# One layer of a graph network on one Trainium2 core: row-sum staging of three slots in place of four

## The chip, the core and the metric

The kernel runs on one core of a Trainium2 chip: TensorE (PE) for matrix products, VectorE (DVE), ScalarE (ACT), GpSimd (POOL), SyncE (SP), which here only issues DMAs, and 16 DMA engines. The metric is the device time of one execution in microseconds, lower is better. In this text 1 MB is 1024 KB, as the profile counts a DMA's size.

## What is computed

```python
# x: 8192 x 128, adj: 8192 x 8192, w: 128 x 128, all float32
A = adj + eye(8192)
d = rsqrt(sum(A, axis=1))
h = (A * d[:, None] * d[None, :]) @ x
x = layernorm(x + elu(h @ w), axis=-1)
```

adj is 256 MB. Its rows have to be summed before d is known, and column t of A can only be used in the product once d_t is known, since x is scaled by it.

## The kernel before, in words

adj is cut into 16 x 16 tiles of 512 x 512 (1 MB). Tile (t, u) holds the columns of band t and the rows of band u. A tile's home is a slot of `space` (line 732): 128 partitions, 4 row blocks (BLOCKS) and 23 slots of 512 columns.

The row bands are taken in order. For band r the strip (columns r to 15 of its rows) is loaded. Together with the tiles to its left, which were loaded earlier as column tiles, it completes the row sums; then d_r follows (`row_sum` on DVE line 1079, `power` on POOL line 914, `scale` on DVE line 1087, copies of the scaled x by turns on DVE 1095 and POOL 932). From then on the column tiles (r, u), u > r, are loaded and used at once. Bands 2 to 11 are HALVED: their d comes in two halves, and a part can be started on the first half of the band.

Of the strip, KEPT says which tiles stay: tile (t, u) is kept for u from t + 1 - KEPT[t] to t. Kept tiles ("near") wait in their slots until d_t is known. The others ("far") are only summed, and are read again at the end ("again"). KEPT sums to 58; 78 tiles are read again, in groups of two row bands (`row_groups`).

Far loads go to the staging area, slots 0 to STAGE - 1. Each of the four row blocks of `space` is one staging row of STAGE x 512 columns (line 812), so with STAGE = 4 a load is 128 rows of 2048 columns: 1 MB, 8 KB contiguous in each row. A strip's odd rest (`part`, line 55) goes in narrower loads. A far load waits until ACT has summed the load that had its staging row before (line 887). Near tiles are loaded in groups of WIDTHS adjacent tiles where so many adjacent slots are free (`near_loads`, line 196), else singly with 2 KB runs. Tiles get slots from STAGE to 22, and the scaled x of a band ("home") takes one such slot too. When all strips are in, the staging slots join them (`close_stage`), and three slots go to the residuals at the end.

Every first-time load is summed by ACT (line 949, one instruction for each row block), every tile is transposed in place by DVE in 32 x 32 squares (line 1072), then multiplied on PE (line 1053) in parts of 1 to 4 tiles of one column band, 128 matmuls for a pair. A part accumulates in one of two PSUM sets; DVE adds it to hT (lines 1106 and 1108). A finished row band gets its product with w (line 1028), ELU and the layer norm.

The order on each engine is written out ahead by `plan()`, a planner that steps through time with fixed costs (line 81 and the `offer` calls): it decides which load is issued next (`next_load`: column tiles go first while fewer than FEED tiles are waiting, strip loads otherwise), which tiles form a part (`next_part`), and which homes stay until the rereads (bands from STAY up; the others are dropped and loaded again). SP issues all loads of adj in this order and waits, one after the other, for the slot or staging row of each. On the chip the engines run at their own pace under semaphores; only the order is the planner's.

Of the kernel before, what the change touches and what calls it, by code (L numbers as in the profile page):

```python
# [5 lines left out]
N = 8192  # L6
F = 128
Q = 4
BAND = 512
BANDS = N // BAND  # L10
BLOCKS = BAND // 128
GROUPS = BAND // 32
SLOTS = 23
STAGE = 4
LATE = 3
KEPT = (1, 2, 3, 4, 5, 6, 5, 4, 5, 4, 5, 4, 1, 2, 3, 4)
AHEAD = 2
STAY = 10
WIDTHS = (4, 2)
XN = 1  # L20
HALVED = range(2, 12)
HALF_JOBS = 2
# [1 line left out]
RING = 4  # L24
SETS = 2
MERGE = 4
FEED = 14
FLIGHT = 4
HOLD = 8
EPS = 1e-5  # L30
# [7 lines left out]
def kept_units():  # L38

    return {(t, u) for t in range(BANDS) for u in range(t + 1 - KEPT[t], t + 1)}  # L40

# [6 lines left out]
def strip_items(r, kept):  # L48

    far = [t for t in range(r, BANDS) if (t, r) not in kept]  # L50
    items = []
    if far:
        assert far == list(range(far[0], BANDS))
        x0 = far[0] * BAND
        part = (N - x0) % 2048
        if part:
            nk = 2048 // part
            items += [("far", r, k, min(nk, BLOCKS - k), x0, part) for k in range(0, BLOCKS, nk)]
        items += [("far", r, k, 1, x, 2048) for x in range(x0 + part, N, 2048) for k in range(BLOCKS)]
    near = sorted((("near", t, r) for t in range(r, BANDS) if (t, r) in kept), reverse=True)  # L60
    if r not in HALVED:
        return items + near
    return items + near + [("split", r), ("rest", r)]
# [14 lines left out]
def plan():  # L78
# [3 lines left out]
    kept = kept_units()  # L82
    loads, tiles, groups = [], [], []
    free = [(0.0, n) for n in range(STAGE, SLOTS)]
    free_rows = [(0.0, n) for n in range(STAGE)]
    homes, tenants = [], [[] for _ in range(SLOTS)]
    order = {e: [] for e in ("sp", "act", "pool", "dve", "pe")}
    ready = {e: [] for e in ("act", "pool", "dve", "pe")}
# [15 lines left out]
    normed = {}  # L104
    counts = {"diagonals": 0, "w": 0, "z": 0, "stored": 0, "outs": 0, "residuals": 0}
    at_row, row_todo, rows_done, stage_open = 0, strip_items(0, kept), False, True
    firsts, queued, rest, backlog = [], [], [], 0
    held_diagonals = {}
# [72 lines left out]
    def drop_home(t):  # L181
        release(homes[home_of.pop(t)][1])
# [13 lines left out]
    def near_loads():  # L196

        left = [v for v in row_todo if v[0] == "near"]
        r, slots = left[0][2], sorted(n for _, n in free)
        for w in WIDTHS:  # L200
            if len(left) < w or len(free) < w + 1 or left[0][1] - left[w - 1][1] != w - 1:
# [31 lines left out]
    def next_load():  # L233
# [15 lines left out]
        if pick_row:  # L249
            pick_row = bool(free_rows) if row_todo[0][0] == "far" else len(free) >= 2  # L250
        if firsts and free and (backlog < FEED or not pick_row):
            t, u = firsts.pop(0)
# [63 lines left out]
    def end_row():  # L316

        nonlocal at_row, row_todo, rows_done, backlog
        if rows_done or any(f[1] == at_row for f in firsts):
            return  # L320
        open_band(at_row)
        if at_row not in HALVED:
            pending_x.append(at_row)
        backlog += sum(1 for v in tiles if v[0] == "first" and v[1] == at_row)
        if at_row + 1 < BANDS:
            at_row += 1
            row_todo = strip_items(at_row, kept)
        else:
            rows_done = True
            close_stage()  # L330

    def close_stage():

        nonlocal stage_open
        if stage_open and rows_done and not far_open:
            stage_open = False
            for slot in range(STAGE):
                tenants[slot].append(("stage", 0))
# [41 lines left out]
    def finished(engine, kind, arg):  # L380
# [48 lines left out]
        elif kind == "part":  # L429
# [4 lines left out]
            for i in these:  # L434
# [4 lines left out]
                else:  # L439
                    again_left[t] -= 1  # L440
            if not first_left[t] and (not again_left[t] or t < STAY and not rows_done):
                drop_home(t)
# [180 lines left out]
def gcn_resnorm(nc: bass.Bass, x: bass.AP, adj: bass.AP, w: bass.AP, out: bass.AP):  # L623
# [3 lines left out]
    AX = mybir.AxisListType  # L627

    loads, tiles, homes, tenants, late, jobs, parts, finals, order, turns, _ = plan()

    def nth_of(engine, kind):
# [90 lines left out]
    with ExitStack() as ctx:  # L722
# [6 lines left out]
        def sem(name):  # L729
            return ctx.enter_context(nc.semaphore(name))  # L730
# [20 lines left out]

        x_loaded = [sem(f"x_loaded{n}") for n in range(XN)]
        w_loaded = sem("w_loaded")
        row_loaded = [sem(f"row_loaded{n}") for n in range(STAGE)]
        loaded = [sem(f"loaded{n}") for n in range(SLOTS)]
        rest_loaded = {n: sem(f"rest_loaded{n[0]}_{n[1]}") for n in sorted({signal_of(v)[1] for v in loads if signal_of(v)[0] == "rest"})}
        res_loaded = [sem(f"res_loaded{n}") for n in range(RING)]
# [46 lines left out]
        def home_of(load):  # L804
# [6 lines left out]
            _, _, _, nk, _, wide, row = load  # L811
            return space[:, row, 0:STAGE].rearrange("p n c -> p (n c)")[:, 0:nk * wide].rearrange("p (k c) -> p k c", k=nk)

# [364 lines left out]
```

## Time and profile before

| | |
|---|---|
| median of 3 runs | 1041.64 us (1041.31 to 1044.76) |
| the profiled execution | 1041.38 us |
| its span | 1039.3 us |
| PE busy | 920.9 us (89%) |
| weight loads | 848.4 us (82%) |
| DVE busy | 788.2 us (76%) |
| ACT busy | 671.4 us (65%) |
| POOL busy | 158.9 us (15%) |
| HBM read | 359.73 MB (here 10^6 bytes), 350 GB/s over the span |

Busy times are of one profiled execution. A busy share over the span says little here, since the kernel has stretches with different limits; the rows further down are read stretch by stretch. An idle time in brackets, as [2.02 <-DVE space L1087], is the time that the engine stood still before the instruction, and what released it.

### The profile page before, as it was taken

To read this page: it belongs to the slowest core of one execution; us is meant where nothing else is said; L and a number is where in the kernel's file an instruction comes from. 1 tells how busy PE (TensorE), PEld (TensorE's weight loads), DVE (VectorE), ACT (ScalarE), POOL (GpSimd) and SP (SyncE) were. 2 spreads that over 40 slices of the span, in tenths; PEclk is the share of its full clock that TensorE was granted. 3 is DMA by queue.
4 is the path that set the end of the run, shared out by engine and by line. 5 is a ranking of instruction groups with operands and counts; after the bars stand their busy time and mean duration, and the time that the engine had idled before them with its cause. 6 is when DMAs were issued, how large, how long until landed. Compare 5 with 4: busy or idle time off the path is not lost.

```text
span 1039.3 us, 35837 instructions
## 1 busy us (share of the span) xinstructions
PE 920.9 (89%) x16128; PEld 848.4 (82%) x16128; DVE 788.2 (76%) x675; ACT 671.4 (65%) x1621; POOL 158.9 (15%) x277
## 2 busy tenths in 40 slices
PE   0099389789798998989999999999999999999995
PEld 0065378679698998989999999999999989999994
DVE  0398298397686968879789877999998978866933
ACT  6888798898889888888888888881213126130201
POOL 0200010300301103030312322344000011000000
PEclk9999789899999999999999999999999999999998
DMA  9999999999999999999999999999899979899920
GB/s 386 401 386 411 402 391 402 396 399 399 378 396 384 386 398 391 384 386 402 382 394 399 390 395 382 386 359 355 288 323 324 305 237 329 283 315 318 347 84 21
DMA packets 168696, 366.23 MB, mean 352 GB/s; under 512 B 6624, under 2 KB 33376, under 8 KB 158816
## 3 DMA queue, kind: packets, MB, share of 16 engines
q1 hardware_dynamic: 151504, 355.49, 92.5%
q10 hardware_dynamic: 17040, 8.46, 2.8%
q8 instruction: 126, 2.06, 0.8%
q14 instruction: 26, 0.21, 0.1%
HBM read 359.73 MB, written 4.19 MB: 350 GB/s over the span
## 4 chain that ended last, share of the span: by engine, by line
PE 63%; DMA 19%; SPq 6%; ACT 5%; DVE 4%; POOL 2%; issue 2%; POOLq 0%; ACTq 0%; DVEq 0%
PE p_set L1053 62%; DMA space<-in_adj 17%; SPq L888 5%; ACT space L949 4%; POOL space L932 2%; DVE space L1072 2%; DMA xn<-in_x 1%; PE p_set L1028 1%; DVE space L1087 1%; SPq L878 1%; POOL d L914 1%; DVE hT L1106 0%; ACT space L980 0%; DVE space L1095 0%; DVE stats L1143 0%
## 5 line engine op out<-in xcount | busy, mean ns | idle before, releaser
L1053 PE MATMUL p_set<-space 32*128 32x256 f32 (+3 forms) x16000 | 905.5, 384 | 106.2 <-DVE space L1072 75.3
L1053 PEld LDWEIGHTS p_set<-space 32*128 32x128 f32 x16000 | 833.5, 187 | 175.8 <-issue 120.0
L949 ACT ACTIVATE space<-space 128x512 f32<-128x512 f32 (+2 forms) x744 | 579.5, 780 | 96.7 <-DMA space<-in_adj 87.2
L1072 DVE STREAM_TRANSPOSE space<-space 128x2048 f32<-128x2048 f32 x256 | 577.2, 2289 | 85.2 <-ACT space L949 55.2
L1106 DVE TENSOR_TENSOR hT<-p_set,hT 128x1024 f32<-128x1024 f32 (+1 forms) x95 | 105.7, 1120 | 98.4 <-PE p_set L1053 98.1
L949 ACT ACTIVATION_READ_ACCUMULATOR space<-space 128x1 f32 x744 | 138.7, 186 | 0.0
L972 ACT ACTIVATE space<-space 128x512 f32<-128x512 f32 x16 | 9.9, 622 | 185.3 <-DVE space L1118 185.3
L914 POOL TENSOR_TENSOR d<-deg,minus_half 128x2 f32<-128x2 f32 (+1 forms) x26 | 20.2, 775 | 550.9 <-DVE deg L1079 550.5
L932 POOL COPY space<-space 32x256 f32<-32x256 f32 (+1 forms) x208 | 94.8, 456 | 27.6 <-DVE space L1087 16.3
L939 POOL TENSOR_TENSOR rstd<-var_eps,minus_half 128x4 f32<-128x4 f32 x16 | 19.1, 1194 | 250.0 <-DVE var_eps L1152 249.9
L957 ACT ACTIVATE space<-space 32x512 f32<-32x512 f32 (+1 forms) x40 | 25.1, 628 | 45.3 <-POOL space L921 40.8
L980 ACT ACTIVATE space<-space,shift,rstd 128x128 f32<-128x128 f32 x60 | 24.7, 482 | 31.6 <-DVE shift L1158 31.6
L1087 DVE TENSOR_TENSOR space<-xn,d 128x256 f32<-128x256 f32 (+1 forms) x26 | 24.8, 954 | 17.7 <-POOL d L914 13.0
L1095 DVE COPY space<-space 64x256 f32<-64x256 f32 (+1 forms) x52 | 20.2, 389 | 1.7
L907 POOL TENSOR_TENSOR space<-space,ident 128x512 f32<-128x512 f32 x16 | 20.4, 1276 | 0.2
L1079 DVE TENSOR_REDUCE deg<-sums 128x2 f32<-128x34 f32 (+1 forms) x26 | 5.0, 191 | 19.5 <-ACT space L949 19.3
L1108 DVE COPY hT<-p_set 128x1024 f32<-128x1024 f32 (+3 forms) x6 | 9.5, 1580 | 11.6 <-PE p_set L1053 11.5
L1028 PEld LDWEIGHTS p_set<-ident,hT 128*128 128x128 f32 x128 | 14.9, 191 | 3.6 <-issue 3.6
L1028 PE MATMUL p_set<-ident,hT 128*128 128x128 f32 x128 | 16.4, 281 | 0.9 <-DVE hT L1106 0.9
L1143 DVE BATCH_NORM_STATS2 stats<-space 128x6 f32<-128x128 f32 x64 | 14.0, 281 | 0.6
L1137 DVE SCALAR_TENSOR_TENSOR space<-space 128x512 f32<-128x512 f32 x16 | 11.0, 689 | 2.2 <-ACT space L974 2.2
L1118 DVE TENSOR_TENSOR space<-p_set,d 128x512 f32<-128x512 f32 x16 | 10.4, 675 | 1.5 <-PE p_set L1028 1.3
(17 smaller groups left out, 40.5 us busy)
## 6 DMA issues: line engine op xcount, KB each, us to landing
space<-in_adj SPq DMA_DIRECT2D x303, 1024.0 KB, 12.6
space<-in_adj SPq DMA_DIRECT2D x50, 512.0 KB, 12.1
space<-in_adj SPq DMA_DIRECT2D x8, 768.0 KB, 13.3
xn<-in_x SPq DMA_DIRECT2D x20, 256.0 KB, 12.1
space<-in_x ACTq DMA_DIRECT2D x16, 256.0 KB, 7.9
out_rows<-space ACTq DMA_DIRECT2D x16, 256.0 KB, 9.9
ident<-in_w ACTq DMA_DIRECT2D x1, 64.0 KB, 5.8
```

The costliest lines, as they stand in the source:

```text
L888: sp.dma_start(home_of(load), source(load)).then_inc(arrival(arg), 16)
L907: nc.gpsimd.tensor_tensor(on_diagonal, on_diagonal, ident[:, :].unsqueeze(1).to_broadcast([128, BLOCKS, 128]), ALU.add)\
L914: nc.gpsimd.tensor_tensor(d[:, r, blocks], deg[:, r % 2, blocks], minus_half[:, blocks], ALU.pow).then_inc(d_ready, 1)
L932: nc.gpsimd.tensor_copy(to, own).then_inc(copied_by["pool"], 1)
L949: ins = nc.scalar.activation(view[:, g], view[:, g], ACT.Copy, accum_out=to[:, g:g + 1])
L957: nc.scalar.activation(to, own, ACT.Copy).then_inc(copied_by["act"], 1)
L980: ins = nc.scalar.activation(pos[:, n % RING, b], pos[:, n % RING, b], ACT.Identity, bias=shift[:, n % RING, b:b + 1], scale=rstd[:, n % R ...
L1028: ins = nc.tensor.matmul(p_set[bank][:, i, F * b:F * (b + 1)], hT[:, at:at + 128], w_sb[:, :], start=True, stop=True)
L1053: ins = nc.tensor.matmul(to, xs_chunk(h, b, turn, q), moving, start=first and not turn and b == blocks_of(half).start, stop=last and turn ...
L1072: nc.vector.transpose(slots[slot], slots[slot]).then_inc(tile_turned, 1)
L1087: nc.vector.tensor_tensor(xs_own(h, half), xn[:, h % XN, blocks], d[:, t, blocks].unsqueeze(2).to_broadcast([128, blocks.stop - blocks.sta ...
L1106: nc.vector.tensor_tensor(rows, new, rows, ALU.add).then_inc(product_added, 1)
```

## The change

STAGE goes from 4 to 3. A far load is then at most 128 x 1536 columns: 768 KB, with 6 KB contiguous in each row. There are still four staging rows, one for each row block; their count was STAGE and is now written as BLOCKS. Slot 3 joins the slots for tiles and homes: 20 in place of 19. With it come other settings: KEPT (sum 61 in place of 58, so 75 tiles are read again), WIDTHS (3, 2), STAY 9 and FEED 12. The order on every engine follows from them by `plan()`.

```diff
--- before.py
+++ after.py
@@ -11,12 +11,12 @@
 BLOCKS = BAND // 128
 GROUPS = BAND // 32
 SLOTS = 23
-STAGE = 4
+STAGE = 3
 LATE = 3
-KEPT = (1, 2, 3, 4, 5, 6, 5, 4, 5, 4, 5, 4, 1, 2, 3, 4)
+KEPT = (1, 2, 3, 4, 5, 6, 6, 4, 5, 4, 3, 4, 5, 6, 1, 2)
 AHEAD = 2
-STAY = 10
-WIDTHS = (4, 2)
+STAY = 9
+WIDTHS = (3, 2)
 XN = 1
 HALVED = range(2, 12)
 HALF_JOBS = 2
@@ -24,7 +24,7 @@
 RING = 4
 SETS = 2
 MERGE = 4
-FEED = 14
+FEED = 12
 FLIGHT = 4
 HOLD = 8
 EPS = 1e-5
@@ -52,11 +52,12 @@
     if far:
         assert far == list(range(far[0], BANDS))
         x0 = far[0] * BAND
-        part = (N - x0) % 2048
+        full = BAND * STAGE
+        part = (N - x0) % full
         if part:
-            nk = 2048 // part
+            nk = full // part
             items += [("far", r, k, min(nk, BLOCKS - k), x0, part) for k in range(0, BLOCKS, nk)]
-        items += [("far", r, k, 1, x, 2048) for x in range(x0 + part, N, 2048) for k in range(BLOCKS)]
+        items += [("far", r, k, 1, x, full) for x in range(x0 + part, N, full) for k in range(BLOCKS)]
     near = sorted((("near", t, r) for t in range(r, BANDS) if (t, r) in kept), reverse=True)
     if r not in HALVED:
         return items + near
@@ -82,7 +83,7 @@
     kept = kept_units()
     loads, tiles, groups = [], [], []
     free = [(0.0, n) for n in range(STAGE, SLOTS)]
-    free_rows = [(0.0, n) for n in range(STAGE)]
+    free_rows = [(0.0, n) for n in range(BLOCKS)]
     homes, tenants = [], [[] for _ in range(SLOTS)]
     order = {e: [] for e in ("sp", "act", "pool", "dve", "pe")}
     ready = {e: [] for e in ("act", "pool", "dve", "pe")}
@@ -751,7 +752,7 @@
 
         x_loaded = [sem(f"x_loaded{n}") for n in range(XN)]
         w_loaded = sem("w_loaded")
-        row_loaded = [sem(f"row_loaded{n}") for n in range(STAGE)]
+        row_loaded = [sem(f"row_loaded{n}") for n in range(BLOCKS)]
         loaded = [sem(f"loaded{n}") for n in range(SLOTS)]
         rest_loaded = {n: sem(f"rest_loaded{n[0]}_{n[1]}") for n in sorted({signal_of(v)[1] for v in loads if signal_of(v)[0] == "rest"})}
         res_loaded = [sem(f"res_loaded{n}") for n in range(RING)]
```

## Rows read from the trace of the kernel before

**Rows 1.** The page's 40 slices: busy tenths of PE, of the DMA engines, and GB/s.
```profile
PE   0099389789798998989999999999999999999995
DMA  9999999999999999999999999999899979899920
GB/s 386 401 386 411 402 391 402 396 399 399 378 396 384 386 398 391 384 386 402 382 394 399 390 395 382 386 359 355 288 323 324 305 237 329 283 315 318 347 84 21
```

**Rows 2.** PE's timeline: start, length, line, form, count, [idle before it <-releaser].
```profile
54.45 57.77 PE L1053 MATMUL p_set<-space 32*128 32x256 f32 x768 [54.45 <-DVE space L1072]
133.09 57.71 PE L1053 MATMUL p_set<-space 32*128 32x256 f32 x896 [20.86 <-DVE space L1072]
196.94 6.49 PE L1053 MATMUL p_set<-space 32*128 32x256 f32 x64 [6.14 <-DVE space L1087]
...
213.36 50.38 PE L1053 MATMUL p_set<-space 32*128 32x256 f32 x896 [3.71 <-issue]
...
393.80 60.80 PE L1053 MATMUL p_set<-space 32*128 32x256 f32 x1088 [2.86 <-DVE space L1087]
456.62 3.01 PE L1053 MATMUL p_set<-space 32*128 32x256 f32 x48 [2.02 <-DVE space L1087]
460.31 48.63 PE L1053 MATMUL p_set<-space 32*128 32x256 f32 x896 [0.69 <-POOL space L932]
509.12 83.16 PE L1053 MATMUL p_set<-space 32*128 32x256 f32 x1536 [0.17 <-POOL space L932]
592.63 146.19 PE L1053 MATMUL p_set<-space 32*128 32x256 f32 x2704 [0.35 <-POOL space L932]
...
838.62 7.19 PE L1053 MATMUL p_set<-space 32*128 32x256 f32 x128 [1.46 <-DVE hT L1106]
...
962.62 62.44 PE L1053 MATMUL p_set<-space 32*128 32x256 f32 x1152
1025.97 2.02 PE L1028 MATMUL p_set<-ident,hT 128*128 128x128 f32 x16 [0.91 <-DVE hT L1106]
```

**Rows 3.** Windows: us, busy PE, PEld, DVE, ACT, POOL, clock, DMA share, GB/s.
```profile
592.50:1028.00 435.50, 433.00 (x7824) 408.53 (x7824) 348.14 (x363) 160.46 (x373) 68.73 (x97) 1.00 0.89 305
...
700.00:1028.00 328.00, 325.63 (x5840) 306.54 (x5832) 254.81 (x290) 69.21 (x139) 33.57 (x37) 1.00 0.84 279
```

**Rows 4.** Timeline of all engines around band 6's second half.
```profile
453.69 0.19 ACT L949 ACTIVATION_READ_ACCUMULATOR space<-space 128x1 f32 x1
453.92 0.19 DVE L1079 TENSOR_REDUCE deg<-sums 128x2 f32<-128x34 f32 x1
454.25 0.70 POOL L914 TENSOR_TENSOR d<-deg,minus_half 128x2 f32<-128x2 f32 x1 [2.81 <-DVE deg L1079]
454.99 1.49 DVE L1087 TENSOR_TENSOR space<-xn,d 128x256 f32<-128x256 f32 x1 [0.88 <-POOL d L914]
```

**Rows 5.** Windows, columns as in rows 3: 8 KB packets, then 2 KB.
```profile
12.00:38.00 26.00, 0.00 (x0) 0.00 (x0) 0.00 (x0) 21.13 (x23) 0.00 (x0) 1.00 1.01 420
...
124.60:148.80 24.20, 15.71 (x208) 12.82 (x212) 21.07 (x14) 22.11 (x70) 7.38 (x10) 0.73 1.05 387
```

**Rows 6.** Loads on line 888: two around 330 us, one around 336.
```profile
L888 SPq DMA_DIRECT2D space<-in_adj x2: 847/1705/2563, 329.4 to 330.3; - x2
DMA to landing us min/median/max: 12.6/13.5/14.4
...
L888 SPq DMA_DIRECT2D space<-in_adj x1: 1417/1417/1417, 336.0 to 336.0; - x1
DMA to landing us min/median/max: 14.3/14.3/14.3
```

**Rows 7.** Loads on line 888: five full staging loads of strip 1, then all rereads.
```profile
DMA to landing us min/median/max: 7.7/7.9/7.9
...
DMA to landing us min/median/max: 5.5/8.7/14.1
```

**Rows 8.** Groups by form: ACT's sums; count, busy us, mean ns, idle before.
```profile
L949 ACT ACTIVATE space<-space 128x512 f32<-128x512 f32 x624 | 384.8, 617 | 56.2 <-DMA space<-in_adj 47.0
L949 ACT ACTIVATE space<-space 128x2048 f32<-128x2048 f32 x76 | 145.2, 1911 | 31.1 <-DMA space<-in_adj 31.1
L949 ACT ACTIVATION_READ_ACCUMULATOR space<-space 128x1 f32 x744 | 138.7, 186 | 0.0
L949 ACT ACTIVATE space<-space 128x1024 f32<-128x1024 f32 x36 | 37.7, 1048 | 8.5 <-DMA space<-in_adj 8.5
L949 ACT ACTIVATE space<-space 128x1536 f32<-128x1536 f32 x8 | 11.8, 1472 | 0.8 <-DMA space<-in_adj 0.6
```

**Rows 9.** Groups by form: the one part of a single tile on PE.
```profile
L1053 PE MATMUL p_set<-space 32*128 32x128 f32 x128 | 3.8, 270 | 0.0
```

**Rows 10.** Loads on line 888: issued from 8 to 23 us, first strip.
```profile
DMA to landing us min/median/max: 6.4/9.0/20.3
```

## The prediction

> **What bounds the kernel now.** The plan, read first, says what has to happen: the 16 row strips are read once (256 tiles of 1 MB), which gives the row sums, and a tile of column band t can only be multiplied once d_t is known. 58 of the 136 tiles on or above the diagonal are kept until then, 78 are only summed and read again. The page's slices come next [rows 1]: the DMA engines are full up to about slice 26 (675 us) and move 380 to 410 GB/s, then less, while PE goes from idle to full. So the kernel has a stretch that the transfers set and one that PE sets, and the question is where the one passes into the other.
>
> PE's timeline gives that place [rows 2]: each idle row of PE is a band boundary at which it had no tile left and waited for the next d. They shrink: 54.45 us at the start, 20.86 at band 1, 6.14, 1.39, 0.69 and 3.71 at band 2, then about 4, 3 and 3, and at band 6 2.02 and 0.69. Behind 460 us there are 0.17 and 0.35, one of 1.46 at 838.62 (PE waits for a PSUM set, not for a tile) and 0.91 before the last product. PE is busy 433.0 of the 435.5 us from 592.5 on [rows 3]. So the end is: the time at which the early strips have come in, plus PE's remaining work, plus 11 us behind the last product. A tile read again costs the end its PE work, not its transfer: during the rereads the DMA engines moved 279 GB/s [rows 3].
>
> PE's work per tile is fixed: nine pairs of tiles in 62.44 us are 3.47 us a tile [rows 2]. Three tiles fewer to read again therefore don't take 3 x 3.47 us off the end; the same three are multiplied earlier instead. They help only as far as they fill idle time of PE.
>
> **Part by part.**
> (1) Tiles per band (15 - t column tiles plus KEPT[t]): before 16 for bands 0 to 5, then 14, 12, 12, 10, 10, 8, 4, 4, 4, 4; after the same 16 up to band 5, then 15, 12, 12, 10, 8, 8, 8, 8, 2, 2. Nothing changes for PE ahead of band 6, where some 101 of its 107 us of idle time lie, paced by transfers. Band 6 gains one tile, (6,1): 3.47 us of work, and a second pair of tiles that can be multiplied on the first half of d_6, ahead of the second half. The wait it would fill is the half-band chain at 451 to 457 us: last sum ends 453.9, row sum 0.19, power 0.70, scale 1.49, and PE starts at 456.62 [rows 4]. What is idle from there to 593 is 2.02 + 0.69 + 0.17 + 0.35 = 3.23 us [rows 2], all less than the 3.47 us added. Gain 3.2 us, floor 0 (if the planner puts the pair elsewhere).
> (2) Strips in 6 KB packets. The far loads go from 80 to 110: 80 of 768 KB, 24 of 512 KB (rows 8 to 13), 3 of 768 KB and 3 of 256 KB in 2 KB packets. 8 KB packets moved 420 GB/s, 2 KB packets 387 [rows 5], which is 2.49 and 2.71 us per MB. For 6 KB: tile (4,7) was issued at 330.28 and landed 14.4 us later, at 344.7; the third of the 768 KB loads behind it was issued at 336.0 and landed at 350.3 [rows 6]. Three loads in 5.6 us is 1.87 us each, 2.49 to 2.51 per MB: the same as 8 KB within 1%. Strips 0 to 5 hold 51 MB of far tiles, 48 of them in 6 KB packets: 48 x 0.01 = +0.5 us, and +0.3 for the odd 2 KB band of strips 0, 4 and 5: +0.8, between 0 and 1.5.
> (3) Groups of three kept tiles instead of four. Before, groups of four appeared in strips 0 to 2 alone (all other kept tiles came singly or in pairs at 2 or 4 KB). Three adjacent free slots are easier to find than four; each group of three saves 3 x (2.71 - 2.50) = 0.6 us of transfer and 3 us of ACT, which has cover. Strips 3, 4 and 5 could have one each, strip 1 two in place of four plus one. I take -0.8 us, between 0 and -1.9. With (2) this is 0.
> (4) Staging in flight. A far load waits until ACT has summed the load that had its row before. Four rows of 1 MB run with 7.9 us from issue to landing and the DMA engines full [rows 7]. With 768 KB the four rows turn in 4 x 1.87 = 7.5 us, of which ACT takes 1.47 + 0.19 [rows 8], leaving 5.8 us from issue to landing. The shortest landing of a whole tile is 5.5 us, with 2.71 of it transfer [rows 7], so a 768 KB load can land in about 4.7. It fits with 1.1 us to spare: cost 0.
> (5) ACT's sums of far blocks: 80 x (1.47 + 0.19) + 24 x (1.05 + 0.19) + 12 x 0.80 = 172 us after, against 170 before [rows 8]. ACT isn't the bound.
> (6) The odd tiles. Column 6 has 15 tiles: one part of three. The last reread group has (6,0) alone, as the very last part. A lone tile costs 3.8 us [rows 9] against 3.47: +0.3.
> (7) Reread groups: 4, 4, 4, 12, 14, 18, 19 tiles instead of 8, 8, 10, 14, 18, 20. Each group end asks DVE to add before the output product. Only one such place cost PE time before (1.46 us [rows 2]); more of them cost 0 to 4.4, I take +0.5.
> (8) STAY 9 keeps the scaled x of band 9, one x load less: nothing while PE leads. FEED 12 only shifts when column tiles go ahead of strip loads.
> (9) The price in slots. Kept tiles plus the homes of bands 9 and up hold slots: at the end of strip 10, 12 kept and 2 homes of 20 (before 9 and 1 of 19); at the end of strip 11, 12 and 3 (before 4 and 2). Only 5 slots are then left for streaming, where 13 were. PE is fed from them while strip 11 lands, and band 11 is also reached earlier (153 tiles precede it, not 154), so it has no slack to spend. At the end of strip 9 the kernel before lives on 7 free slots without a gap. I take 0, bounds 0 and +7 (two tiles' work).
>
> Sum on the profiled execution: -3.2 + 0 + 0 + 0.3 + 0.5 = -2.4. The profiled execution took 1041.38 us, its span 1039.3, the median of the runs is 1041.64: forecast 1039.2.
>
> The Trainium skill (DMA: Bandwidth & Descriptors, Bandwidth and Rules for kernel authors) speaks against smaller loads: at least 1 MiB per DMA, and a fixed 2 us for each. The rows above set the step from 1 MB to 768 KB at 2.49 - 1.87 = 0.62 us, a quarter of the load, so nothing fixed shows while loads queue. By the page's fixed part in full, 30 loads more would cost an estimated 60 us.
>
> **Rivals.**
> (a) The streaming slots run out (part 9). PE waits at bands 10 to 12 for tiles that can't be loaded because kept ones hold the slots. For: 5 slots cover 5 x 3.47 = 17 us, and the near tiles of strip 11 with the d chain take about 15. Against: PE is behind the transfers by a few us there. It decides once that stretch exceeds 17 us; price 3.5 to 9 us: 1042.5 to 1048. This is the case that ends slower.
> (b) Staging starves (part 4). If landing needs the 6.4 us that was the shortest in the first strip [rows 10], the four rows turn in 8.1 us instead of 7.5, 0.15 us a load; over the 64 whole far loads of strips 0 to 5 that is 9.6 us, all on the path: 1045 to 1049. Against: most far loads stand between tile loads that cover them.
> (c) Early strips come quicker: the three-wide groups form everywhere and less of the odd loads shows; another 1.5 to 4 us: 1035 to 1037.5.
> (d) The gap is not filled or moves to the next band: no change, 1041 to 1042.
> (e) A fixed cost per load does show: by the shortest landings about 2.8 us, exposed for each far load that is added, 30 x 2.8 = 84 us: 1125.
>
> **How the numbers follow.** About 0.3% (3.1 us) is what a measurement here can tell from no change. Forecast case (1036.5 to 1041) 0.45, of which 0.18 below 1038.5; (a) 0.17, of which 0.12 above 1044.8; (b) 0.08; (c) 0.13, of which nearly all below; (d) 0.14; (e) 0.03. Faster 0.18 + 0.13 + 0.02 = 0.33; slower 0.12 + 0.07 + 0.03 = 0.22; same 0.45. The range 1034.5 to 1047 leaves out (e), the far ends of (b) and (c) and the worst of (a).
>
> **What would show it.** PE's gaps up to band 5 as before within 2 us; no gap at band 6; matmul pitch unchanged; a far stretch at 415 to 420 GB/s with landings near 5.8 us. Wrong if PE has gaps between 590 and 700 us (then a), if the first product or band 1 comes more than 1 us later (b), or if the band gaps ahead of band 6 shrink.

## The result, and the profile after

The kernel after takes 1044.99 us (median), the kernel before 1041.90 in the same comparison; the ratio is 1.003, with a 95% interval of 1.0021 to 1.0039. It is slower by 0.3%, some 3.1 us, where 1039.2 was forecast: inside the range, on the other side of "before". All ratios in this text are of undisturbed executions; one of 2814.92 us with seven rows and one of 1467.42 us with the early table are not among them. The profiled execution took 1044.75 us, its span 1043.0. Lines of the kernel after are one higher than those of before (matmuls L1054, sums L950, loads L889, transposes L1073, scale L1088).

The page's slices of after, as in [rows 1]:

```profile
PE   0089479689798999999999999999999999999995
DMA  9999999999999999999999999989989988999920
GB/s 344 404 387 375 409 389 389 395 397 396 376 383 395 385 397 384 376 393 392 384 385 389 384 389 388 389 305 287 339 299 322 347 296 260 318 307 302 337 99 21
```

The first slice moves 344 GB/s where it moved 386. PE has an 8 in the third slice where it had a 9; from slice 14 on it has no digit under 9 but the last slice's, where before still had an 8 in slices 16 and 18. PE's timeline of after, columns as in [rows 2]:

```profile
56.99 58.38 PE L1054 MATMUL p_set<-space 32*128 32x256 f32 x768 [56.99 <-DVE space L1073]
137.00 57.72 PE L1054 MATMUL p_set<-space 32*128 32x256 f32 x896 [21.63 <-DVE space L1073]
201.85 6.00 PE L1054 MATMUL p_set<-space 32*128 32x256 f32 x64 [7.13 <-DVE space L1088]
209.92 5.38 PE L1054 MATMUL p_set<-space 32*128 32x256 f32 x64 [2.07 <-DVE space L1088]
...
399.88 7.15 PE L1054 MATMUL p_set<-space 32*128 32x512 f32 x64 [1.79 <-DVE space L1088]
407.22 103.02 PE L1054 MATMUL p_set<-space 32*128 32x512 f32 x1648 [0.19 <-DVE space L1088]
510.45 1.15 PE L1054 MATMUL p_set<-space 32*128 32x256 f32 x16 [0.21 <-POOL space L933]
512.84 3.00 PE L1054 MATMUL p_set<-space 32*128 32x256 f32 x48 [1.24 <-DVE space L1088]
516.52 45.18 PE L1054 MATMUL p_set<-space 32*128 32x256 f32 x832 [0.68 <-POOL space L933]
562.14 73.67 PE L1054 MATMUL p_set<-space 32*128 32x256 f32 x1360 [0.44 <-POOL space L933]
636.16 124.44 PE L1054 MATMUL p_set<-space 32*128 32x256 f32 x2048 [0.36 <-issue]
1029.58 2.05 PE L1029 MATMUL p_set<-ident,hT 128*128 128x128 f32 x16 [1.41 <-DVE hT L1107]
```

Against [rows 2]: the first product is 2.5 us later (54.45 to 56.99), band 1 3.9 us (133.09 to 137.00), band 2 4.9, band 5 6.1 (393.80 to 399.88); the end of the last product is 3.6 us later (1027.99 to 1031.63). So the change loses 6.1 us by band 5 and gives 2.5 back behind it. There is no row at band 6 any more. The two windows that this cuts, columns as in [rows 3], first of the kernel before:

```profile
0.00:393.80 393.80, 292.33 (x4737) 256.00 (x4737) 266.25 (x166) 335.44 (x789) 43.32 (x85) 0.95 1.03 394
393.80:1028.00 634.20, 628.59 (x11392) 592.43 (x11392) 514.54 (x481) 331.97 (x825) 113.16 (x190) 1.00 0.93 332
```

and of the kernel after:

```profile
0.00:399.88 399.88, 294.28 (x4736) 260.70 (x4737) 267.27 (x166) 337.46 (x805) 43.24 (x85) 0.94 1.02 388
399.88:1031.60 631.72, 627.19 (x10880) 575.90 (x10880) 513.46 (x488) 326.31 (x839) 112.14 (x189) 1.00 0.93 328
```

Of the 6.1 us ahead of band 5, 4.1 are idle time of PE (393.80 - 292.33 = 101.5, then 399.88 - 294.28 = 105.6) and 2.0 are longer busy time for the same matmuls, at a mean granted clock of 0.94 instead of 0.95 (both are means over stretches at 2.4 and at 1.2 GHz). The transfers of that stretch run at 388 instead of 394 GB/s. Where they fall behind shows at once. The window of 8 to 13 us, first before, then after:

```profile
8.00:13.00 5.00, 0.00 (x0) 0.00 (x0) 0.00 (x0) 5.00 (x10) 0.00 (x0) 1.00 1.01 419
```

```profile
8.00:13.00 5.00, 0.00 (x0) 0.00 (x0) 0.00 (x0) 4.39 (x10) 0.00 (x0) 1.00 0.86 306
```

The fifth load of after waits for ACT's sums of the first. ACT's timeline of after shows when those are done:

```profile
5.61 1.28 ACT L950 ACT_TABLE_LOAD   x1 [5.61 <-DMA space<-in_adj]
6.91 0.63 ACT L950 ACTIVATE space<-space 128x512 f32<-128x512 f32 x1
...
8.66 0.19 ACT L950 ACTIVATION_READ_ACCUMULATOR space<-space 128x1 f32 x1
...
13.32 1.48 ACT L950 ACTIVATE space<-space 128x1536 f32<-128x1536 f32 x1 [0.93 <-DMA space<-in_adj]
```

The first load lands at 5.6 us, the table costs 1.28, three sums of 512 columns follow, and the row is free at 8.85; the fifth load is issued at 8.9 and lands at 13.3, some 3.3 us behind the fourth instead of 1.9. Before, the fifth load was issued later still (9.2), but three rows of 1 MB were in flight behind the first (in after 256 KB and twice 768) and it landed on the beat of 2.49 us. A later stretch, of strip 1's staging loads, shows the same; 97 to 106 us, first before, then after:

```profile
97.00:106.00 9.00, 9.00 (x132) 6.42 (x128) 4.47 (x2) 7.08 (x8) 0.00 (x0) 1.00 1.01 419
```

```profile
97.00:106.00 9.00, 9.00 (x112) 5.64 (x108) 2.90 (x2) 7.43 (x10) 0.00 (x0) 1.00 0.98 369
```

There ACT starts its sums of whole rows 1.87 us apart with one interval of 2.29 in after (98.56 to 100.85 us), and 2.48 apart throughout in before.

The lack shows in the waits of SP's queue too. Queue, line, whom it waited for: us in total, times, longest; before, then after:

```profile
SPq L888 <- PE p_set L1053: 424.2, 94, 8.9
SPq L888 <- ACT space L949: 91.3, 44, 11.2
```

```profile
SPq L889 <- PE p_set L1054: 398.3, 88, 9.9
SPq L889 <- ACT space L950: 151.4, 66, 10.8
```

SP waits 60 us more for a sum to free a staging row, and ACT in turn waits 100.3 instead of 87.2 us for a landing. The HBM reads fell from 359.73 to 356.32 MB: 3.15 for the three tiles that are no longer read again, and 0.26 for band 9's x, which is loaded once less (here 10^6 bytes).

### The profile page after: what moved, and what is told of

Read it like the earlier page. It is cut to its first block, busy times and chain, and to the rows that moved or that the text cites. A ratio compares the mean times of both kernels' runs of the same rounds, so it can differ in the third digit from the quotient of the medians.

```text
span 1043.0 us, 34873 instructions
## 1 busy us (share of the span) xinstructions
PE 921.5 (88%) x15616; PEld 836.6 (80%) x15616; DVE 788.1 (76%) x682; ACT 667.8 (64%) x1651; POOL 157.8 (15%) x276
## 3 DMA queue, kind: packets, MB, share of 16 engines
HBM read 356.32 MB, written 4.19 MB: 346 GB/s over the span
## 4 chain that ended last, share of the span: by engine, by line
PE 72%; DMA 14%; SPq 5%; ACT 3%; DVE 2%; POOL 2%; issue 2%; ACTq 0%; POOLq 0%; DVEq 0%
PE p_set L1054 70%; DMA space<-in_adj 14%; SPq L889 4%; ACT space L950 3%; PE p_set L1029 2%; POOL space L933 1%; DVE space L1088 1%; DVE space L1073 1%; POOL d L915 1%; SPq L879 0%; DVE hT L1107 0%; ACT space L981 0%; DVE stats L1144 0%; DVE space L1138 0%; DVE deg L1080 0%
## 5 line engine op out<-in xcount | busy, mean ns | idle before, releaser
L1054 PE MATMUL p_set<-space 32*128 32x256 f32 (+3 forms) x15488 | 906.1, 392 | 108.7 <-DVE space L1073 78.6
L1054 PEld LDWEIGHTS p_set<-space 32*128 32x128 f32 x15488 | 821.7, 188 | 190.9 <-issue 132.8
L950 ACT ACTIVATE space<-space 128x512 f32<-128x512 f32 (+2 forms) x764 | 582.9, 764 | 110.6 <-DMA space<-in_adj 100.3
L1073 DVE STREAM_TRANSPOSE space<-space 128x2048 f32<-128x2048 f32 x256 | 577.2, 2289 | 92.9 <-ACT space L950 54.8
L1107 DVE TENSOR_TENSOR hT<-p_set,hT 128x1024 f32<-128x1024 f32 (+2 forms) x102 | 108.6, 1079 | 89.3 <-PE p_set L1054 88.8
L950 ACT ACTIVATION_READ_ACCUMULATOR space<-space 128x1 f32 x764 | 142.5, 187 | 0.0
L958 ACT ACTIVATE space<-space 32x512 f32<-32x512 f32 (+1 forms) x30 | 18.8, 628 | 59.7 <-POOL space L922 57.7
L1088 DVE TENSOR_TENSOR space<-xn,d 128x256 f32<-128x256 f32 (+1 forms) x26 | 23.3, 895 | 16.6 <-POOL d L915 12.7
L1109 DVE COPY hT<-p_set 128x1024 f32<-128x1024 f32 (+2 forms) x6 | 9.4, 1568 | 15.4 <-PE p_set L1054 15.4
L922 POOL TENSOR_TENSOR space<-xn,d 128x512 f32<-128x512 f32 x3 | 3.5, 1162 | 61.2 <-DMA xn<-in_x 61.2
```

Of the source, the lines that this page charges most:

```text
L950: ins = nc.scalar.activation(view[:, g], view[:, g], ACT.Copy, accum_out=to[:, g:g + 1])
L1054: ins = nc.tensor.matmul(to, xs_chunk(h, b, turn, q), moving, start=first and not turn and b == blocks_of(half).start, stop=last and turn ...
L1073: nc.vector.transpose(slots[slot], slots[slot]).then_inc(tile_turned, 1)
L1088: nc.vector.tensor_tensor(xs_own(h, half), xn[:, h % XN, blocks], d[:, t, blocks].unsqueeze(2).to_broadcast([128, blocks.stop - blocks.sta ...
L1107: nc.vector.tensor_tensor(rows, new, rows, ALU.add).then_inc(product_added, 1)
```

## The experiments

The theory is rival (b): four rows of 768 KB leave the transfers without work, because a row comes free too late. Its opponents are the odd loads alone, ACT's late start, the order that the planner writes, and a price of the smaller load itself. Times are in us; "band 5" is the start of its first matmul on PE.

Each ratio is to executions of before in the same comparison; the other columns are of one profiled execution each.

| kernel | ratio to before, 95% | first product | band 1 | band 5 | last product ends | last - band 5 |
|---|---|---|---|---|---|---|
| before | 1 | 54.5 | 133.1 | 393.8 | 1028.0 | 634.2 |
| after | 1.003 (1.0021 to 1.0039) | 57.0 | 137.0 | 399.9 | 1031.6 | 631.7 |
| after, nine rows in strip 0 | 0.9999 (0.999 to 1.0008) | 55.2 | 134.6 | 397.3 | 1028.7 | 631.4 |
| after, seven rows everywhere | 0.9967 (0.9956 to 0.9978) | 55.1 | 133.4 | 395.4 | 1026.5 | 631.1 |
| before, six rows | 0.9997 (0.9983 to 1.0011) | 54.6 | 133.4 | 393.7 | 1028.5 | 634.8 |
| after, three rows | 1.042 (1.0401 to 1.0439) | 62.3 | 147.6 | 425.1 | 1072.0 | 646.9 |
| before, three rows | 1.0081 (1.0063 to 1.01) | 58.2 | 140.3 | 402.2 | 1036.8 | 634.6 |
| after, table early | 1.0014 (1.0001 to 1.0027) | 56.4 | 136.3 | 398.7 | 1029.7 | 631.0 |
| before, table early | 0.9999 (0.9986 to 1.0011) | 54.4 | 133.1 | 393.3 | 1028.0 | 634.7 |
| after, nine rows and table early | 0.9999 (0.9988 to 1.0011) | 55.2 | 134.6 | 397.5 | 1028.7 | 631.2 |
| after, nine rows, other costs | 1.0002 (0.9988 to 1.0015) | 55.2 | 135.2 | 398.1 | 1031.4 | 633.3 |
| after, odd part last | 1.0023 (1.001 to 1.0036) | 55.3 | 135.1 | 398.0 | 1032.5 | 634.5 |

### Nine rows in the first strip

```
+ROWS = 9
+    first_far = [k for k, load in enumerate(loads) if load[:2] == ("far", 0)]
+    for n, k in enumerate(first_far):
+        loads[k] = loads[k][:6] + (n % ROWS,)
...
+            if row >= BLOCKS:
+                at = BAND * STAGE * (row - BLOCKS)
+                return hT[:, at:at + nk * wide].rearrange("p (k c) -> p k c", k=nk)
```

> The changed kernel, but the far loads of strip 0 alternate over nine staging rows (four as before, five in hT, which nothing uses until the first product is added). Depth theory (four rows of 768 KB let the transfers run dry in strip 0): the first product comes 1.5 to 2.5 us earlier than the changed kernel's 56.99 us, every band start up to band 5 moves by as much, and the end too: 1042.5 to 1043.5 us. Packet theory (6 KB packets are slower by themselves): nothing moves, 1045. Order theory (the loss comes from the order and the narrow loads, not from waiting for staging rows): nothing moves, 1045.

Measured: 1042.03 us beside 1041.66 of before, ratio 0.9999. The window of 8 to 13 us is full again:

```profile
8.00:13.00 5.00, 0.00 (x0) 0.00 (x0) 0.00 (x0) 5.00 (x11) 0.00 (x0) 1.00 1.02 422
```

The first product is 1.8 us earlier than in after, band 5 2.6, the last product 2.9. Rows in one strip alone take back nearly the whole of the 3.1 us, a little more than expected (1042.5 to 1043.5). The kernel is then even with before, not ahead of it. Of the 6.1 us at band 5 they take back 2.6.

### Three rows, in both kernels

Each far load also waits for the sum of the far load three before it.

```
+    fars = [k for k, load in enumerate(loads) if load[0] == "far"]
+    row_third = {k: fars[n - 3] for n, k in enumerate(fars) if n >= 3}
...
+                if load[0] == "far" and row_third.get(arg) is not None:
+                    sp.wait_ge(act_summed, sum_nth[row_third[arg]])
```

> The changed kernel with one more wait: each far load also waits until the far load three before it is summed, so three are in flight at most instead of four; order and sizes unchanged. Depth theory: a 768 KB load takes 4.4 us to land on idle DMA engines and 1.7 us to be summed, so three rows give one load in 2.05 us at best instead of 1.88; band 5 starts 5 to 12 us later than 399.9 and the end moves with it: 1050 to 1057 us. Packet and order theory: within 1.5 us of 1045.

> The kernel before with the same added wait: three far loads of 1 MB in flight, 3 MB, as many bytes as four of 768 KB. Depth theory, in bytes: it loses about what the changed kernel lost before band 5, 3 to 6 us, so 1044 to 1048 us, and PE's gap at band 6 stays. Packet and order theory: within 1 us of 1041.9.

Measured: after 1085.7 us, ratio 1.042; before 1050.44 us, ratio 1.0081. The sign is that of the depth theory in both. The size was foreseen in neither: before was expected at 1044 to 1048 us, after at 1050 to 1057, and after's loss of 41 us is over four times that of before. PE's timeline of after with three rows, and its window of 8 to 13 us:

```profile
62.28 57.31 PE L1058 MATMUL p_set<-space 32*128 32x256 f32 x768 [62.28 <-DVE space L1077]
147.61 57.40 PE L1058 MATMUL p_set<-space 32*128 32x256 f32 x896 [28.01 <-DVE space L1077]
217.75 6.44 PE L1058 MATMUL p_set<-space 32*128 32x256 f32 x64 [12.74 <-DVE space L1092]
```

```profile
8.00:13.00 5.00, 0.00 (x0) 0.00 (x0) 0.00 (x0) 2.86 (x8) 0.00 (x0) 1.00 0.63 222
```

So the kernel after stands on a slope where one row less costs 4%, and the kernel before nearer to its foot. By the table 25.2 us of after's loss lie ahead of band 5 and 15.2 behind it, where PE goes on waiting at band boundaries up to 673 us; before loses 8.4 and 0.4. Why the wait lasts so long in after wasn't traced.

Before on three rows also tests whether bytes alone count, since it has 3 MB in its rows as after has on four. It loses 8.4 us at band 5, where 3 to 6 were expected and after itself lost 6.1.

### The staging cycle by itself

All but the cycle is left out: SP issues far loads of one width into so many rows, ACT sums each over its row, and SP waits for a sum to free a row. Six stretches, each given by width, rows and number of loads:

```
PHASES = ((2048, 4, 24), (1536, 4, 32), (1536, 5, 32), (1536, 3, 32), (2048, 3, 24), (1024, 4, 48))
...
                if ahead:
                    sp.wait_ge(summed, ahead)
                sp.dma_start(stage[:, r, 0:wide], adj[128 * row:128 * row + 128, col:col + wide]).then_inc(landed[r], 16)
...
                act.wait_ge(landed[r], many)
                nc.scalar.activation(stage[:, r, 0:wide], stage[:, r, 0:wide], ACT.Copy, accum_out=sums[:, k:k + 1]).then_inc(summed, 1)
```

> Only the staging cycle, nothing else of the kernel: loads of 128 rows, each summed by ACT, each waiting for the sum of the load that had its row. Six stretches one after the other: 2048 columns with 4 rows (24 loads), 1536 with 4, 5 and 3 rows (32 each), 2048 with 3 rows (24), 1024 with 4 rows (48). The output is not computed. Depth theory: 2.49 us a load; 1.88 to 1.95; 1.88; 2.05 to 2.3; 2.5 to 2.6; 1.3 to 1.5. Packet theory: 1536 columns take over 1.92 us with 4 and with 5 rows alike. Order theory: 1.88 with 4 rows, so that the cycle by itself loses nothing.

Its windows, one for each stretch in that order (busy ACT and POOL, clock, DMA share, GB/s):

```profile
1.00:62.00 61.00, 46.91 (x47) 0.00 (x0) 1.00 1.00 413
66.00:128.00 62.00, 48.06 (x61) 0.00 (x0) 1.00 1.00 405
132.00:193.00 61.00, 48.63 (x61) 0.00 (x0) 1.00 1.00 412
196.00:273.00 77.00, 48.52 (x61) 0.00 (x0) 1.00 0.91 327
276.00:348.00 72.00, 45.92 (x46) 0.00 (x0) 1.00 0.95 349
352.00:426.00 74.00, 52.90 (x93) 0.00 (x0) 1.00 0.97 340
```

The mean interval between landings and the median time from issue to landing in the steady part of each stretch:

| load | rows | us per load | us per MB | issue to landing |
|---|---|---|---|---|
| 1 MB | 4 | 2.50 | 2.50 | 7.9 |
| 768 KB | 4 | 1.935 | 2.58 | 6.2 |
| 768 KB | 5 | 1.884 | 2.51 | 7.8 |
| 768 KB | 3 | 2.44 | 3.25 | 5.7 |
| 1 MB | 3 | 3.01 | 3.01 | 7.1 |
| 512 KB | 4 | 1.555 | 3.11 | 5.1 |

The smaller load has no price: with five rows 768 KB cost per MB what 1 MB does. With four rows it lags by 0.05 us a load, as an interval of 2.2 to 2.4 us at every sixth or seventh load among regular ones of 1.88. With three it takes 2.44. The stretches with full depth came as expected; those on three rows came slower (expected 2.05 to 2.3 for 768 KB, 2.5 to 2.6 for 1 MB), as did 512 KB (1.3 to 1.5). And bytes in the rows are not the whole measure: 3 MB as three rows of 1 MB cost 3.01 us per MB, as four rows of 768 KB 2.58. Landings of the steady 768 KB cycle on three and on four rows, from issue:

```profile
DMA to landing us min/median/max: 4.4/5.7/6.4
...
DMA to landing us min/median/max: 5.9/6.2/6.4
```

On three rows the DMA engines are idle for 9% of the time, and still the landing takes 5.7 us. A row's turn is that plus ACT's 1.66 us: 7.4, and 3 x 2.44 is 7.3. Four rows at full speed leave 4 x 1.884 = 7.5 us. So there were 0.2 us to spare, not 1.1.

### Seven rows in all strips

The staging rows of all strips are seven. To make room hT is cut to seven bands: left out is that the products land in their own places and that the product with w reads them (it reads w instead).

```
+    for n, k in enumerate([k for k, load in enumerate(loads) if load[0] == "far"]):
+        loads[k] = loads[k][:6] + (n % 7,)
...
-        hT = sb("hT", [128, N])
+        hT = sb("hT", [128, 7 * BAND])
+        spare = sb("spare", [128, 3, BAND * STAGE])
```

> The changed kernel with its order and sizes, but with seven staging rows in place of four in all strips. The room comes from hT, which is cut to 7 x 512 columns: sums of different row bands fall on each other and the product with w reads w itself, so the output is wrong while every instruction keeps its size and place. Depth theory: nothing waits for a staging row any more; the band starts fall back to those of the kernel before (band 1 at 133, band 3 at 268 to 269, band 5 at 393.5 to 395 us, where the changed kernel had 399.9), no gap of PE at band 6, and the end is the kernel before less the gaps filled behind band 5, 1038.5 to 1040 us, as the prediction's sum has it. Remaining-mix theory (strip 0 apart, where nine rows brought 3 us, the rest of the delay is from the order, 2 KB pieces and narrow loads): band 5 stays at 396.5 to 397.5 and the end at 1041.5 to 1042.5 us.

Measured: 1039.43 us beside 1043.30 of before, ratio 0.9967 (0.9956 to 0.9978).

```profile
55.12 56.96 PE L1058 MATMUL p_set<-space 32*128 32x256 f32 x768 [55.12 <-DVE space L1077]
133.36 57.17 PE L1058 MATMUL p_set<-space 32*128 32x256 f32 x896 [21.28 <-DVE space L1077]
...
395.36 7.15 PE L1058 MATMUL p_set<-space 32*128 32x512 f32 x64 [1.50 <-DVE space L1092]
```

```profile
SPq L894 <- ACT space L955: 73.8, 45, 8.6
```

Band 1 is back at 133.4 us, band 5 at 395.4 (before 393.8, after 399.9), and SP's wait for sums is 73.8 us, with 11.7 more on the added rows (after: 151.4). The span is 1037.8 us where the sum of the prediction gave 1036.9 (before's 1039.3 - 2.4). With the cycle deep enough the change would be worth what the prediction's sum promised, but the room for these rows came from hT, which the whole kernel needs. The window of 97 to 106 us moves 415 GB/s here (after 369, before 419; nine rows in strip 0 alone 390).

### Six rows in the kernel before

The control for it: the same cuts, rows of 1 MB.

```
+    for n, k in enumerate([k for k, load in enumerate(loads) if load[0] == "far"]):
+        loads[k] = loads[k][:6] + (n % 6,)
```

> The control: the kernel before with six staging rows of 1 MB in place of four, made by the same cut of hT (output wrong in the same way). Depth theory: four rows of 1 MB already keep the transfers full, so band 5 starts within 1 us of 393.8 and the end is within 1 us of 1041.9. If it came down by 2 us or more, the staging depth would be a cost of both kernels, and the comparison with seven rows would have to be read against it.

Measured: ratio 0.9997, every band start within 0.4 us of before, the last product 0.5 later. Four rows of 1 MB lose nothing, and the cuts in hT gain nothing by themselves; so the gain of seven rows is that of depth. (The cuts by themselves were tried on the order of before only.)

### The order that the planner writes

The kernel with nine rows in strip 0, planned with other costs for loads.

```
-    FAR, MID, NEAR, XLOAD, LAND = 2.57, 2.65, 2.73, 1.0, 2.0
+    FAR, MID, NEAR, XLOAD, LAND = 2.57, 2.57, 2.73, 1.0, 2.5
```

> The changed kernel with nine rows for strip 0 (as in the run before that brought it to 1042.0) and the order planned anew with two of the planner's own costs nearer to the traces: 2.57 for 1 MB in 6 KB runs in place of 2.65, and 2.5 us in place of 2.0 from the end of a transfer to its use. Depth theory: the order changes when far loads come, not how deep they stand, so the strips still lose 3 us to dry spells; a better cover could give back 1 to 3 us: 1039 to 1042 us. If order alone were the cause, it should change the end by 5 us or more either way.

Measured: 1043.39 us, ratio 1.0002 (0.9988 to 1.0015). Band 5 is at 398.1 instead of 397.3 and the last product 2.7 us later in the profile. PE stands idle for 2.71 us at band 7, where it did for 1.26 and 0.68 without the new costs. An order made with costs nearer to the traces wins nothing; other orders weren't tried.

### ACT's table ahead of the first sum, in both kernels

```
+        warm = sb("warm", [128, 1])
...
+            nc.scalar.activation(warm[:, :], sums[:, 0, BANDS:BANDS + 1], ACT.Copy)
```

> The changed kernel with one tiny ACT instruction ahead of all, so that the 1.28 us load of ACT's table is over before the first tile lands. Depth theory: the first sums end 1.3 us earlier, the first waiting far load is issued at 7.6 instead of 8.9 us, and the hole of 1.4 us in the landings of strip 0 closes: first product and end 1.0 to 1.4 us earlier, 1043.6 to 1044.2. Packet and order theory: no change, 1045.

> The kernel before with the same tiny activation ahead of ScalarE's first sum. It has four rows of 1 MB, and six of them brought nothing, so the depth theory expects that the wait of the fifth load for the first sum costs it nothing and the early table brings nothing either: a ratio of 0.999 to 1.001, first product at 54.3 to 54.6 us. If ScalarE's late start costs a kernel something whatever the size of its loads: a ratio of 0.998 and a first product at 53.5.

ACT's timeline of after with it:

```profile
0.74 1.28 ACT L996 ACT_TABLE_LOAD   x1 [0.74 <-PEq L1172]
...
5.54 0.63 ACT L951 ACTIVATE space<-space 128x512 f32<-128x512 f32 x1 [3.25 <-DMA space<-in_adj]
```

Measured: after 1.0014 (1.0001 to 1.0027) with the first product 0.6 us earlier; before 0.9999, its first product 0.1 us earlier. After gains less than the 1.0 to 1.4 us expected. By the profiles, the 1.28 us that ACT starts sooner are worth something only in the kernel that is short of rows. The interval of after with the table early overlaps that of after, so this gain is likely, not settled.

### Nine rows and the early table together

> The kernel after with both repairs: the first strip's staging cycles through nine rows (five of them in the output buffer hT, which nothing reads before the phases), and ScalarE runs one tiny activation before its first sum, so that its table is in place when the first slot lands. With nine rows in the first strip no load waits for the first sum before the tenth, so the depth theory expects the 1.28 us of the table to be hidden already and this kernel to stand with the one that has nine rows alone: 1041.5 to 1042.5, first product at 55.0 to 55.3 us. If the two gains were independent they would add: 1040 to 1041, a ratio of 0.998 to the kernel before. If ScalarE's start, not the row, sets the first strip: first product at 53.5 to 54.

Measured: 0.9999 (0.9988 to 1.0011), first product 55.2 us: as with nine rows alone. The two gains don't add, since they are one: the wait for the first sums. This version, like nine rows alone, is even with before; no version that computes the whole was faster than before.

### The odd part behind the whole ones

```
-        if part:
+        if part and r:
...
+        if part and not r:
+            nk = full // part
+            items += [("far", r, k, min(nk, BLOCKS - k), x0, part) for k in range(0, BLOCKS, nk)]
```

> The kernel after with one edit: in the first strip the odd column part of two tiles (the 512 KB loads) is staged behind the whole ones, where the kernel after has it ahead of them. The depth theory: the rows hold whole slots of 768 KB for as long as the strip fills, a 512 KB load in one of four rows no longer lowers the bytes in flight at the start; the first product comes 0.3 to 1.0 us earlier than in the kernel after (57.0), the time 1044 to 1045. If the small loads at the start are what costs, and not the depth in the steady cycle: the first product at 55 to 55.5 and the time with that of the nine rows, 1042.

(The odd column part is in fact one load of 768 KB, three blocks of 512 columns, and one of 256 KB, not two of 512 KB.) Measured: 1044.36 us, ratio 1.0023 (1.001 to 1.0036). The first product comes at 55.3 us, 1.7 earlier than in after, where the depth theory had 1.0 at most: the position of the odd loads makes most of the first strip's loss, as the other theory of this run had it (55 to 55.5), though its 1042 us didn't come. I read it as still a matter of rows, in a form that I hadn't costed; the run doesn't separate the two. The first load is now one sum of 1.48 us in place of three of 512 columns, so that its row is free 0.8 us earlier, and no row holds 256 KB while the queue fills. The ACT timeline and the window of 8 to 13 us:

```profile
6.44 1.48 ACT L953 ACTIVATE space<-space 128x1536 f32<-128x1536 f32 x1
7.83 0.19 ACT L953 ACTIVATION_READ_ACCUMULATOR space<-space 128x1 f32 x1
```

```profile
8.00:13.00 5.00, 0.00 (x0) 0.00 (x0) 0.00 (x0) 4.41 (x7) 0.00 (x0) 1.00 0.99 380
```

Band 5 keeps this lead (398.0 against 399.9), but the end doesn't: it takes 634.5 us from there to the last product, not 631.7. The windows of 505 to 553 us show PE's granted clock at 0.86, behind an idle 1.94 us at band 7, and then DMA engines at 0.91:

```profile
505.00:530.00 25.00, 22.49 (x359) 20.61 (x355) 20.07 (x16) 21.62 (x65) 8.32 (x18) 0.86 1.05 389
530.00:553.00 23.00, 23.00 (x436) 22.20 (x432) 17.91 (x13) 17.94 (x41) 3.90 (x9) 1.00 0.91 337
```

In after the clock there was 1.00. Finer windows put the granted clock at 0.50 (1.2 GHz) from 513 to 517 us, right behind the 1.94 us of idle time, and back at 1.00 from 520. From the end of the first 16 matmuls of band 7 to the end of its block this kernel takes 52.7 us, after 50.1: 2.6 of the 2.8 us. The idle time in it is the same (1.94 against 1.24 and 0.68); the same 880 matmuls are busy 50.7 us instead of 48.2. That the clock took the gain is what this one trace shows; no run tested it.

## Why the prediction was right or wrong

**What bounds the kernel.** Right. Up to band 5 the transfers set the time, behind it PE's work does, and what was lost in the first part came through to the end: 6.1 us lost and 2.5 gained behind it are the 3.6 us of the last product. What was lost early was not absorbed by a wait later: seven rows bring band 5 4.5 us forward and the last product 5.1.

**Part 4, staging in flight, is the step that failed.** It put the landing that a 768 KB load needs at 4.7 us, by scaling the shortest landing in the trace, and so found 1.1 us to spare in a turn of 7.5. The cycle by itself shows 5.7 us at the median where it runs dry; the shortest, 4.4, is no guide to what a cycle gets load after load. Rightly sized, the step gives 7.5 - 1.66 - 5.7 = 0.2 us to spare, which any unevenness uses up. Measured it is 0.05 us a load in the steady cycle; over the 52 whole far loads of strips 1 to 5 that is 2.7 us. The difference between after and seven rows agrees: 4.5 us at band 5, of it 1.9 at the first product, so 2.6 behind it. That the two sizes meet is partly luck, since other loads stand between the far ones, and which loads paid wasn't traced; that depth is the cause rests on the runs with more rows.

**What part 4 didn't have.** Of the 6.1 us at band 5 2.5 sit at the very start, which the step didn't look at: the first turn of the rows includes ACT's table (1.28 us), the three sums of the odd load, and a row that carries 256 KB. Only the term for a steady cycle was formed. Of the 2.5 us at the first product, more rows give back 1.8 and the odd part behind the whole ones 1.7.

**Rival (b)** named this mechanism and the sign that it would show by ("the first product or band 1 more than 1 us later"), with a landing of 6.4 us and 9.6 us as its gross price; the landing measured is 6.2, the loss 4.5 by the seven rows. Its counter-argument, that other loads cover most far loads, holds only in part. On three rows the cycle alone loses 0.5 us a load in both kernels; by the planner's lists strips 0 to 5 hold 64 whole far loads after and 40 before, an estimate of 32 and 20 us, and the kernels lost 25.2 and 8.4 at band 5. At 0.08 its chance was too low: with a bound of 6.4 us from [rows 10] against 4.7 of my own scaling, both ends of an unknown landing were on the table, 5.8 was the point that decides, and it lies between them. This should have been near an even chance, and the forecast with it nearer to no change.

**Parts 2 and 3, the packets.** Right as a price: 1.884 us for 768 KB in the cycle with enough rows, 1.87 predicted; 2.50 for 1 MB, 2.49 predicted. So rival (e) is out. The Trainium skill (DMA: Bandwidth & Descriptors, Anatomy of one DMA) puts a fixed cost of about 2 us on each DMA, fitted on DMAs that GpSimd issues; while these loads, which SP issues, queue, none shows: 2.51 and 2.50 us per MB. What the smaller load costs here is the depth: with the same number of rows each turn of the rows is shorter, and the landing doesn't shrink by as much. The advice of the Trainium skill (DMA: Bandwidth & Descriptors, Rules for kernel authors), at least 1 MiB per DMA, fits the result, but with five rows the cycle shows no loss at 768 KB. Some 1.6 us at band 5 remain between before and seven rows (393.8 and 395.4): 0.3 at band 1 (133.1 and 133.4), 1.2 at band 2 (196.9 and 198.2); whether they come from the groups of three or from the new order of loads is open.

**Part 1, the gap at band 6.** The gap of 2.02 and 0.69 us is gone, as said, but a smaller one opened at band 7: 0.21, 1.24 and 0.68. With 0.44 and 0.36 that makes 2.93 us of idle time from band 6 to the last product's approach, where before had 3.23. The term was sized at -3.2 and is worth -0.3: this is rival (d), the gap that moves to the next band. Band 7 has 12 tiles in both kernels, and seven rows, with the strips on time, show the gap too (0.99 and 0.68). PE reached band 7's boundary at 510.2 us, only 1.3 us later than before (508.9) though it began band 5 6.1 us later. Nothing in the working asked whether band 7's d would be ready for a PE that no longer waits at band 6.

**Parts 6 and 7.** The wait for a PSUM set (1.46 us) didn't multiply with the group ends, it disappeared; the one ahead of the last product grew from 0.91 to 1.41. Together -1.0 instead of part 7's +0.5. Part 6's lone tile cost 0.1 instead of 0.3: the last block takes 59.11 us, where eight pairs at 6.94 and one tile at 3.47 are 59.0.

**Busy time that no term had.** PE was busy 1.4 us less behind band 5 (628.59 and 627.19). The opening of band 5 alone makes up for it. There before's first 17 tiles of [rows 2] take 60.80 us, where 17 x 3.47 is 59.0; their first 39 matmuls, up to 397 us, run at a granted clock of 0.50 (1.2 GHz), after's opening at 1.00. But before with the table early has 1.00 there too, and its same 17 tiles again take 60.8 us from first to last, 0.87 of them now idle (0.69 and 0.18). So at least half of this "busy" time was a wait in another form. After, which opens the band with four tiles in one part, has 0.19 us idle there; that this is why is not shown.

**The sum.** So the sum -2.4 met the measured -2.5 (634.2 and 631.7) by terms that were wrong in both directions. Five of the kernels built on the change take 631.0 to 631.7 us for this stretch, the four built on before 634.2 to 634.8: the gain is real, its parts were not those of the working. That the sum met it is luck. The three others that take longer are the one with other costs (633.3), the one with the odd part last (634.5) and the one with three rows (646.9).

**Parts 5, 8 and 9.** ACT never became the bound; its sums only matter as the part of a turn. No idle time between 590 and 700 us beyond 0.36 (and 107.64 of 108 us busy in 592 to 700): the five streaming slots sufficed, rival (a) is out, as is (c).

## What to carry to other kernels

- When a ring of buffers changes its slot size, cost the turn, not the transfer: rows x transfer time must exceed the landing of a load in a cycle that runs dry, plus the consumer's time. Here 7.5 us against 7.4 (768 KB, four rows) lost 0.05 us a load, and 10.0 against 9.2 (1 MB, four rows; 7.1 and 2.1) lost nothing.
- Take the landing from a cycle by itself with one row less, at its median, not from the shortest in the trace (and not from a full cycle: 7.8 us at 768 KB on five rows, where loads queue), and work out the first turn apart: it holds the consumer's late start and its odd first loads.
- A gap that is filled at one boundary can open at the next: here 2.71 us closed at band 6 and 2.13 opened at band 7. Ask when the next wait ends for an engine that comes earlier before counting it as gained.

## What was unexpected of the hardware

- How steep it gets: the step from four rows to three costs 1.0081 at 1 MB and 1.042 against 1.003 at 768 KB. By itself the cycle goes from 2.50 to 3.01 us and from 1.935 to 2.44 us a load, nearly the same 0.5 us; the difference between the two kernels isn't in the cycle alone.
- The landing of a load shrinks less than in proportion to its size: in cycles that run dry 7.1 us at 1 MB, 5.7 at 768 KB, and 5.1 at 512 KB on four rows, against 2.5 and 1.9 us that a load takes in a full cycle of the first two sizes.
- A cycle that is short by little doesn't slow evenly: five or six intervals of 1.88 us and then one of 2.2 to 2.4.
